# Last layer: gathering the sparse heads' tokens with three bf16 parts in place of one fp32 tile

## What is computed

```python
def _mosa_branch(X, router_w, wqkv, wo):
    b, t, _ = X.shape
    k = t // SPARSITY                                   # 512 // 8 = 64
    scores = jnp.einsum('bth,hn->bnt', X, router_w)
    _, idx = jax.lax.top_k(scores, k)
    idx = jnp.sort(idx, axis=-1)
    gates = jax.nn.sigmoid(jnp.take_along_axis(scores, idx, axis=-1))
    Xg = jnp.take_along_axis(X[:, None], idx[..., None], axis=2)
    qkv = jnp.einsum('bnkh,hnd->bnkd', Xg, wqkv)
    ...
return _mosa_branch(...) + _dense_branch(...)
```

## Time and profile before

| | |
|---|---|
| median of the runs | 501.42 us (500.17, 501.42, 501.61) |
| the profiled execution | 503.28 us, of which the profile's span is 501.5 us |
| mean granted TensorE clock | 0.986 of full speed |
| TensorE matmuls | 455.6 us busy, 91% of the span |
| TensorE weight loads | 281.7 us |
| VectorE, ScalarE, GpSimd | 280.1 us (56%), 220.8 us (44%), 111.9 us (22%) |
| DMA | 32 GB/s on average |

### The profile page before, as it was taken

How to read it: one execution, slowest core, us unless ns; L and a number is a source line. 1 busy time by engine, 2 the same in 40 slices (tenths; PEclk the granted TensorE clock), 3 DMA queues, 4 the chain that set the end, 5 groups by cost and what they waited for, 6 DMA issues and landing times.

```text
span 501.5 us, 7786 instructions
## 1 busy us (share of the span) xinstructions
PE 455.6 (91%) x3075; PEld 281.7 (56%) x3080; DVE 280.1 (56%) x588; ACT 220.8 (44%) x442; POOL 111.9 (22%) x98
## 2 busy tenths in 40 slices
PE   6999999889999899987999999989889989899986
PEld 3534434485776445676754775765345544666552
DVE  3656785446555664787225663653567752465561
ACT  3155566332212164444233324532378755467460
POOL 1300000310101012554000006000255551394300
PEclk9999999979999999999899999999999999899999
DMA  8800000360000000000000002000011110111000
GB/s 297 338 2 1 2 1 0 109 215 0 2 1 0 1 0 2 0 2 2 1 0 0 1 2 84 1 1 0 1 21 23 23 21 15 30 23 22 1 21 22
DMA packets 5493, 16.17 MB, mean 32 GB/s; under 512 B 1489, under 2 KB 2386, under 8 KB 4946
## 3 DMA queue, kind: packets, MB, share of 16 engines
q1 hardware_dynamic: 5458, 15.68, 10.0%
HBM read 13.06 MB, written 0.52 MB: 27 GB/s over the span
## 4 chain that ended last, share of the span: by engine, by line
PE 67%; DVE 18%; issue 6%; ACT 4%; POOL 3%; DMA 1%; SPq 0%; DVEq 0%; ACTq 0%; POOLq 0%
PE PS L537 58%; PE PS L798 2%; PE PS L1160 2%; DVE mxd L2173 2%; DVE mx L1747 2%; DVE wmoe L1740 2%; POOL rstd L2376 2%; PE PS L565 2%; ACT wmoe L1581 1%; DVE keys L1865 1%; DMA cols<-cols_dram 1%; PE PS L626 1%; ACT PT L1414 1%; DVE PS L2166 1%; POOL wmoe L2406 1%
## 5 line engine op out<-in xcount | busy, mean ns | idle before, releaser
L2376 POOL TENSOR_TENSOR rstd<-veps,mhalf 128x4 f32<-128x4 f32 x16 | 16.4, 1034 | 241.5 <-DVE veps L1685 241.5
L537 PE MATMUL PS<-PTB,keys 128*64 128x128 f32 (+3 forms) x384 | 41.2, 377 | 0.0
L1581 ACT ACTIVATE wmoe<-PS,mxd 128x512 f32<-128x512 f32 (+3 forms) x64 | 33.2, 535 | 4.7 <-DVE mxd L2173 4.5
L1593 ACT COPY PTB<-PS 128x768 f32<-128x768 f32 (+1 forms) x24 | 20.9, 873 | 23.8 <-PE PS L1160 23.6
L1865 DVE TENSOR_REDUCE keys<-PS 128x9 f32<-128x693 f32 x32 | 26.5, 871 | 8.6 <-PE PS L537 8.6
L537 PE MATMUL PS<-cst 128*128 128x512 f32 (+2 forms) x66 | 30.0, 566 | 0.4 <-DVE x L1705 0.4
L537 PE MATMUL PS<-va,PT 128*128 128x72 f32 (+2 forms) x224 | 28.4, 277 | 0.9 <-ACT PT L1414 0.9
L537 PEld LDWEIGHTS PS<-PTB,keys 128*64 128x64 f32 (+2 forms) x384 | 20.7, 145 | 14.5 <-issue 11.6
L1359 ACT ACTIVATE sq<-PS 128x512 f32<-128x512 f32 x16 | 9.6, 599 | 43.0 <-PE PS L537 43.0
L537 PEld LDWEIGHTS PS<-va,PT 128*128 128x128 f32 (+1 forms) x224 | 26.4, 191 | 3.0 <-ACT PT L1414 2.0
L537 PE MATMUL PS<-keys,PTB 32*128 32x231 f32 (+2 forms) x448 | 27.1, 327 | 0.3 <-DVE wmoe L1761 0.3
(11 more groups left out here) (349 smaller groups left out, 954.5 us busy)
## 6 DMA issues: line engine op xcount, KB each, us to landing
wmoe<-w_dram SPq DMA_DIRECT2D x2, 2048.0 KB, 12.1
den<-wmoe SPq DMA_DIRECT2D x28, 64.0 KB, 2.3
wa<-wa_dram SPq DMA_DIRECT2D x4, 256.0 KB, 13.2
wlate<-ew_dram SPq DMA_DIRECT2D x2, 512.0 KB, 5.7
wd<-wd_dram SPq DMA_DIRECT2D x1, 1024.0 KB, 9.1
wlate<-wm_dram SPq DMA_DIRECT2D x1, 1024.0 KB, 4.7
cst<-const_dram SPq DMA_DIRECT2D x1, 754.5 KB, 8.0
cst<-const_dram SPq DMA_DIRECT2D x1, 551.0 KB, 5.5
```

The lines of the kernel that those rows point to most:

```text
L537: return nc.tensor.matmul(o, l, r, start=start, stop=stop, skip_group_check=True)
L1581: A_(PR[n % 2][:, z, to:to + (t + 1) * 128], PS[:, ring_banks("turn", n).start + z, to:to + (t + 1) * 128], ACT.Exp, bias=mxd[:, n % 2, k, ...
L1593: nc.scalar.copy(PTR[n % 2][:, :, 0:width], PS[:, 4:6, 0:width]).then_inc(S("d_turned"), 1)
L2376: g.tensor_tensor(rstd[:, b, :], veps[:, b, :], mhalf[:], ALU.pow).then_inc(S("ln_rstd"), 1)
```

## The change

`tparts[b]` names three bf16 tiles of 128 x 512 for each batch, in buffers that are no longer used by then (`wqk0`, `sw2`, `mbias`, `wf1`). A new function `split(b)` in GpSimd's `final_layer` makes them of `htok`: the tokens rounded to bf16 (`hi`), the rest written back over `htok`, that rounded to bf16 (`mid`), and what then remains (`lo`). The three add up to the fp32 value. `split(0)` stands ahead of `rope(1)`, `split(1)` behind `rope(2)`. Each of its four operations waits for the one before it. TensorE's `gather` waits for the parts (`sp_parts`) and takes twelve bf16 matmuls in place of four fp32 ones.

```diff
@@ TensorE, sparse(b, s)
                     elif s == "gather":
                         pe.wait_ge(S(f"sp_G{b}"), TB - b)
-                        for t in range(TB):
-                            last = mm(PS[:, 7, :], htok[:, b * TB + t, :], OH[b][:, t, :], start=(t == 0), stop=(t == TB - 1))
+                        pe.wait_ge(S("sp_parts"), 4 * (b + 1))
+                        for n, part in enumerate(tparts[b]):
+                            for t in range(TB):
+                                last = mm(PS[:, 7, :], part[:, t * 128:(t + 1) * 128], OH[b].bitcast(BF16)[:, t, 1:1024:2],
+                                          start=(n == 0 and t == 0), stop=(n == 2 and t == TB - 1))
@@ GpSimd, final_layer
+                def split(b):
+
+                    hi, mid, lo = tparts[b]
+                    tokens = htok[:, b * TB:(b + 1) * TB, :].rearrange("p t f -> p (t f)")
+                    pool.wait_ge(S("sp_htok"), b + 1)
+                    g.tensor_copy(hi, tokens).then_inc(S("sp_parts"), 1)
+                    pool.wait_ge(S("sp_parts"), 4 * b + 1)
+                    g.tensor_tensor(tokens, tokens, hi, ALU.subtract).then_inc(S("sp_parts"), 1)
+                    pool.wait_ge(S("sp_parts"), 4 * b + 2)
+                    g.tensor_copy(mid, tokens).then_inc(S("sp_parts"), 1)
+                    pool.wait_ge(S("sp_parts"), 4 * b + 3)
+                    g.tensor_tensor(lo, tokens, mid, ALU.subtract).then_inc(S("sp_parts"), 1)
+
+                split(0)
                 for r in range(1, PAIRS):
                     rope(r)
+                    if r == 2:
+                        split(1)
                     if r == 5:
                         sparse_rope()
```

More of the change, by code:

```diff
@@ L432, in build @@
         tab = C3("tab").bitcast(BF16)
+        early = wqk0[:].rearrange("p z r -> p (z r)")
+        tparts = [[early[:, 256 * b:256 * b + 256].bitcast(BF16), (sw2[:].rearrange("p j d -> p (j d)"), mbias[:].rearrange("p t k -> p (t k)")[:, 0:256])[b].bitcast(BF16),
+                   (early[:, 512:768], wf1[:].rearrange("p n d -> p (n d)")[:, 0:256])[b].bitcast(BF16)] for b in range(B)]
         turns = C3("turns", 0, PLACED).bitcast(BF16)
```

## The result

The changed kernel takes 499.34 us (median of 22 executions), the kernel before 501.50 (22 executions, among them the three shown above). The ratio is 0.9954 with a 95% interval of 0.9933 to 0.9975: faster by 0.46%. On a second chip it was 498.70 against 502.48, ratio 0.9927 (0.9898 to 0.9955). Forecast were 499.5 us, with a range of 497.4 to 501.7, and faster as the likeliest outcome (0.56). Medians in this document are those of all executions, while ratios, mean clocks and times at full speed leave out four executions (three of the kernel before, one of e1) that stand far above the rest or over 1.5% above the fastest of their kernel.

The account below looks back on a forecast made before the run. TensorE's stream, with two fp32 gathers on the path to the end, was taken as the bound. Saving 1.9 us there, all else costing nothing, turned the 501.42 us median into 499.5 (503.28 in the profile into 501.4); range 497.4 to 501.7.

Parts of the forecast that it names:

- The term for the gathers: TensorE's two gathers: 2.67 us each in bf16 in place of 3.63 and 3.60, saving 1.89 us.
- the bounds of 1.53 and 2.07: Both gathers' saving in us, with all twelve matmuls at the angles' mean (0.24) or all at 0.215.
- the inner rate: Last eight matmuls of each new gather: 0.215 us each, taken from the expert layer's bf16 gather.
- one sign: On TensorE, `angles` was to start 0.9 to 1.0 us earlier after the first gather's start.
- The rate of the Trainium skill: About 131 ns a matmul, making a gather 1.6 us and the saving about 4 us; the forecast went by the trace instead.
- Cost nothing, from either bound: GpSimd's `split(0)`, 3.6 to at most 6.6 us, fits the 7.2 us of room before anything moves.
- The new wait: TensorE's wait for GpSimd's parts (`sp_parts`) ahead of the gathers: costs nothing, with over 20 us of cover.
- B: Rival at the two gathers: stepped bf16 matmuls go at the fp32 pace, 0.43 us each, giving 504.9 us; chance 0.04.
- D: Rival at the gathers: bf16 matmuls overlap one another, 0.11 us a step, saving 4.4 us, giving 497.1; chance 0.01.
- C: Rival between the gathers: TensorE waits for ScalarE's copies and half the gain is lost, 500.5 us; chance 0.10.
- A: Clock rival, TensorE's pause behind turn 11: no fall gives 497.7 us (chance 0.12), one more fall 501.3 (0.14).
- Nothing: VectorE beside `split(1)`: no cost, as `MATCH_REPLACE8` takes 0.67 us with GpSimd busy or idle.

Follow-up runs that it names:

- e1: Changed kernel with GpSimd's eight new operations kept but the gathers put back to fp32; 502.11 us, 0.9997 of the kernel before.
- e0: The changed kernel run once more without any edit, on a second chip; 498.70 us against 502.48 for the kernel before.
- e3: Changed kernel with one-hots written as bf16 side by side, read without a step; 497.93 us, 0.9912 of the kernel before.
- e2: Changed kernel without the third bf16 part, eight matmuls a gather in place of twelve; 498.70 us, 0.9918 of the kernel before.
- e9: Changed kernel with two idle fp32 matmuls ahead of the first bf16 gather; 501.09 us, 0.9984 of the kernel before.
- e12: Kernel before with fp32 gathers that leave out the last of four token blocks; 499.19 us, 0.9942 of the kernel before.

## Why the prediction was right

*The number.* 499.5 forecast, 499.34 measured, and the mechanism is the one given: TensorE streams shorter gathers on the path that sets the end, and what follows moves with it. That the two agree to 0.2 us is luck. The term for the gathers was 0.27 us too large, and the clock, which the sum left out, gave more than that: at full speed the gain is 1.3 +- 0.2 us, by medians 2.2 and 3.8.

*TensorE's term, slightly mis-sized.* Forecast 2.67 us a gather, measured 2.81; saved 1.62 us and not 1.89. It lies within the bounds of 1.53 and 2.07. By fours a gather was to take 0.95 + 0.86 + 0.86; e0 has 0.91 + 0.91 + 0.99. Two steps failed. One is the inner rate: I took the expert layer's 0.215 for the eight inner matmuls and read the angles' 0.95 for four as one uncovered load and three such steps. With the stepped operand the rate is 0.225 (e3 gives 0.215 without the step), and the trace before had it: taken record by record, the first two of the angles' matmuls start at 413.80 and 414.06, the last at 414.52 and the next work at 414.75, so that the first step is 0.26 and the last 0.23. The other is the end: some 0.10 is spent on the way to the fp32 work behind the gather, and the sum had nothing for it. The fp32 gather showed that too. I put all of its 0.16 to 0.19 down to the uncovered first load, but its last record starts at 412.42 and the next work at 412.94, 0.52 in place of 0.43: about half of it lies at the end. For the same reason one sign was missed: `angles` was to start 0.9 to 1.0 us earlier behind the first gather's start, and starts 3.66 us behind it in place of 4.49, 0.83 earlier. The rate of the Trainium skill, 131 ns a matmul ("TensorE: Matmul & The Clock Gate", section "Back-to-back issue gap"), did not appear in these gathers: no pair there went below 0.215.

*GpSimd.* Forecast 4 us for each `split`, measured 359.06 to 362.82 and 386.40 to 390.18, 3.8 each, with the casts at 0.61 (bound 0.52 to 1.64) and the subtractions at 1.16. "Cost nothing, from either bound" is shown by e1.

*The new wait.* The parts were there at 362.8 and 390.2, the gathers asked at 409 and 414.7. No wait of TensorE names GpSimd there.

*Rivals.* B (the fp32 pace for stepped bf16, 0.43 us) and D fall by the rate itself, C by the 0.88 us that stayed and by e2. A is half right. It happened in the profile: no fall at the pause. Over all executions the mean clock rose by 0.0027 +- 0.0006, about 1.4 us. At full speed the gain is 1.3 +- 0.2 us, which is no clear difference from the 1.62 in the trace. On e0's chip alone it is 1.6 +- 0.4 at full speed and about 1.6 of clock (0.9898 against 0.9866), of 3.8 by medians. On the chip of the result the clocks of the kernel before are not on record, and how its 2.2 us divide is open. The ratios of the two chips differ by no more than their intervals allow. My number left the clock out, and on the second chip it would have been 0.8 us too high. One fall that does not come was worth 1.5 us in the profile, where I had 1.8. Why the clock is higher with the change is not settled: neither the length of the stretch (e9) nor the kind of matmul (e12) is shown to be the cause, and filling the pause raises it in the one kernel and not in the other.

*What I overlooked.* I wrote for VectorE: "Nothing", after two rows of one operation that agree. I had looked beside `split` only, and at one kind of operation. GpSimd does hold VectorE up elsewhere, in both kernels, for 1.6 to 2.2 us of VectorE's time. It does not touch the sum, because it was there before; but the base I summed from was the one profile in ten without it, and so the span fell by 1.8 us only although the clock gave some 1.5.

## What to carry to other kernels

Where fp32 matmuls with 0/1 operands lie on the critical path, three bf16 parts in 12 matmuls at 0.225 us beat four fp32 ones at 0.86 by a fifth (2.81 us against 3.6), if an idle engine can make the parts; lay the one-hots side by side and it is a little more. A copy from SBUF to SBUF on VectorE beside a busy GpSimd is worth moving to ScalarE when ScalarE idles. And where one profile is the base, compare its waits with a second one before an effect is charged to a change: two things of 1.5 us each, a held copy and a fall of the clock, came and went here between executions. The clock was higher with the change by more than its error, but nothing here says why, so that part of the gain is not to be counted on elsewhere.

## What the hardware showed that I had not expected

- VectorE's copy of 512 fp32 columns from SBUF to SBUF takes 0.43 us alone and 2.01 to 2.58 us when a GpSimd operation of 2.4 us has just begun, and then ends 0.28 or 0.29 us behind it (nine profiles); where both began together (one profile), the copy took its 0.43 and GpSimd's operation 2.70 in place of 2.42. VectorE's `MATCH_REPLACE8` takes 0.67 us in either case. The Trainium skill, "SBUF — State Buffer", section "Who interferes with whom", has it so: copies in a two-port mode and GpSimd take turns at a shared port, whole instructions at a time, and whoever is first wins. The traces agree in both orders, the second seen once; that this copy runs in such a mode no run here shows.
- bf16 matmuls of 512 columns whose moving operand is every second element run at 0.225 us, with neighbouring elements at 0.215 (the change and e3).
- About 0.10 us more passes between the last of a gather's matmuls and the fp32 work with operands of 64 rows or columns behind it, for bf16 gathers (0.99 and 0.96 for the last four, in place of 0.90 and 0.86) as for fp32 ones (0.52 in place of 0.43). It does not come with every change to fp32: between the angles' last matmul and the transposes of 128x128 behind it lie 0.23 (before). No run shows what the 0.10 is spent on.
- GpSimd's subtraction of 512 columns takes 1.16 us with a bf16 operand; its operation on two fp32 tiles of that size in the earlier trace rows, of another kind, takes 1.26.
